# Turning a tile's normalised rows with transposing transfers in place of TensorE

## The reference

```python
def block(x, ...):                       # x: (2, 4096, 512) float32
    h = layernorm(x)                     # time mix
    k, r = h @ Wk.T, h @ Wr.T
    y = wkv_scan(-exp(time_decay), time_first, k, r)   # recurrence along the 4096 steps
    x = x + (sigmoid(r) * y) @ Wo.T
    z = layernorm(x)                     # attention and experts
    h = rmsnorm(z, gamma1)
    q = (h @ Wq + bq).reshape(b, t, 16, 32)
    kv = ((h @ Wdown + bdown) @ Wup + bup).reshape(b, t, 16, 64)
    att = softmax(q . k / sqrt(32))      # over the 16 heads of one token
    z = z + (att @ v) @ Wo2 + bo
    h2 = rmsnorm(z, gamma2)
    gate = softmax(h2 @ Wg + bg)         # 8 experts, all of them used
    return x + z + sum_e gate[e] * (h2 @ We[e])
```

## Time and profile before

| what | value |
|---|---|
| median of 3 runs | 2760.3 us (2759.11 to 2760.59) |
| the profiled execution's own time | 2758.6 us |
| its span, first to last instruction | 2756.5 us |
| TensorE busy | 2586.4 us (94%) |
| VectorE busy | 2133.6 us (77%) |
| ScalarE busy | 1531.3 us (56%) |
| GpSimd busy | 948.9 us (34%) |
| mean granted TensorE clock | 0.975 of full |
| queue of the transfers | 116.18 MB in 845,092 packets, 22.9% of the 16 engines' span |

### The profile page before, as it was taken

One profiled execution on the slowest core, in us unless ns is written; L12 is line 12 of the kernel. 1 busy time (PEld: TensorE's weight loads), 2 busy tenths in 40 slices (PEclk: granted clock), 3 DMA queues, 4 the chain that ended last, 5 costly groups with the idle time before them and its releaser, 6 DMA issues.

```text
span 2756.5 us, 48625 instructions
## 1 busy us (share of the span) xinstructions
PE 2586.4 (94%) x18896; PEld 1580.4 (57%) x18896; DVE 2133.6 (77%) x3647; ACT 1531.3 (56%) x2799; POOL 948.9 (34%) x970
## 2 busy tenths in 40 slices
PE   2458999999999999999999999999999999999999
PEld 2345566666556666655666665566666556655554
DVE  6677887788888778788877878887787888767743
ACT  5875555555555555555555555556555555654540
POOL 0453433333333333243333324333332433332420
PEclk7768999999999999999999999999999999999999
DMA  7202222211222221122222112222112222201220
GB/s 229 39 12 39 47 47 47 32 27 37 47 47 47 47 30 28 38 47 47 47 47 25 33 38 47 47 47 47 23 33 40 47 47 47 46 12 37 39 32 16
DMA packets 845322, 119.29 MB, mean 43 GB/s; under 512 B 813587, under 2 KB 813715, under 8 KB 845075
## 3 DMA queue, kind: packets, MB, share of 16 engines
q1 hardware_dynamic: 845092, 116.18, 22.9%
HBM read 48.49 MB, written 16.78 MB: 24 GB/s over the span
## 4 chain that ended last, share of the span: by engine, by line
PE 88%; DVE 4%; ACT 4%; POOL 2%; SPq 1%; issue 1%; DMA 0%; ACTq 0%; DVEq 0%; POOLq 0%
PE bank L1333 78%; PE bank L1355 3%; PE bank L1500 2%; PE bank L1471 2%; PE bank L1511 2%; DVE h2t L1104 1%; PE bank L1487 1%; POOL w_e L693 1%; ACT h2t L939 1%; PE bank L1512 1%; ACT ot L789 1%; DVE mcol L1234 0%; ACT t L888 0%; POOL pr L734 0%; DVE acc L1311 0%
## 5 line engine op out<-in xcount | busy, mean ns | idle before, releaser
L1333 PE MATMUL bank<-w_e,h2t 128*128 128x512 f16 x6144 | 1383.4, 380 | 2.8 <-DVE acc L1311 2.0
L1333 PEld LDWEIGHTS bank<-w_e,h2t 128*128 128x128 f16 x6144 | 592.1, 98 | 665.9 <-issue 4.4
L1311 DVE SCALAR_TENSOR_TENSOR acc<-bank,gates,acc 128x512 f32<-128x512 f32 x512 | 371.9, 736 | 120.4 <-PE bank L1333 117.4
L906 ACT ACTIVATE pr<-bank,plog,col 128x512 f32<-128x512 f32 x256 | 198.7, 776 | 407.9 <-PE bank L1500 405.5
L734 POOL TENSOR_TENSOR pr<-pr 128x512 f16<-128x512 f32 x256 | 295.7, 1160 | 182.3 <-ACT pr L908 180.9
L721 POOL TENSOR_TENSOR qo<-t,qo 128x256 f16<-128x256 f32 x128 | 106.5, 832 | 493.4 <-ACT qo L891 490.3
L1142 DVE TENSOR_TENSOR_SCAN wkv<-e,wkv 128x256 f32<-128x256 f32 x256 | 210.8, 864 | 74.6 <-ACT e L834 73.4
L1166 DVE RECIPROCAL zz<-zz 128x256 f32<-128x256 f32 x128 | 218.9, 1732 | 29.4 <-POOL zz L703 29.3
L1333 PE MATMUL bank<-w_o,xo 128*128 128x512 f16 x768 | 176.2, 387 | 46.9 <-DVE xo L1104 46.9
L908 ACT ACTIVATE pr<-bank,plog,col 128x512 f16<-128x512 f32 x256 | 197.8, 773 | 0.0
L1333 PE MATMUL bank<-xo,w_k 128*128 128x256 f16 x1536 | 172.9, 273 | 2.4 <-DVE xo L1104 2.4
(11 more groups left out here) (196 smaller groups left out, 3957.6 us busy)
## 6 DMA issues: line engine op xcount, KB each, us to landing
qs<-qo SPq DMA_DIRECT2D x384, 64.0 KB, 2.4
ks<-k SPq DMA_DIRECT2D x384, 64.0 KB, 2.4
xk<-in_attn_x SPq DMA_DIRECT2D x32, 512.0 KB, 4.0
x<-in_attn_x SPq DMA_DIRECT2D x32, 512.0 KB, 3.7
result<-acc SPq DMA_DIRECT2D x32, 512.0 KB, 2.8
w_e<-in_ffn_We SPq DMA_DIRECT2D x7, 1024.0 KB, 12.9
qs<-in_attn_Wk SPq DMA_DIRECT2D x1, 1024.0 KB, 7.9
ks<-in_attn_Wr SPq DMA_DIRECT2D x1, 1024.0 KB, 10.0
```

The costliest lines, as they stand in the source:

```text
L906: nc.scalar.activation(pr[:, k % 2, :], att_bank[ATT_BANK["S", k]][:, :], ACT.Exp, bias=plog[:, 0:1], scale=colof["soft"])\
L1311: V.scalar_tensor_tensor(out=acc[:, s, :], in0=moe_bank[u % 2][:, :], scalar=gates[:, s, e:e + 1], in1=acc[:, s, :], op0=ALU.mult, op1=ALU ...
L1333: ins = nc.tensor.matmul(dst, left(a), right(b), start=(n == 0), stop=(n == last))
```

## The change

For time mix and attention, TensorE's turn goes. The rows are split first, while tokens are on partitions: ScalarE writes the high half of each 128 rows and VectorE the low half, into `row16` (the storage of `v32`) and `hr16` (the storage of `k16`). SyncE then issues one transposing transfer for each half of each 128 rows, 4 for `mix_turn` and 4 for `att_turn`, 128x512 float16 (128 KB) each, from there to `xo16` and `ht16`. `mix_k` and `att_latent` on TensorE wait for the transfers (`turn_in`, `turn1_in`) and not for the low half. The turn of the second norm (`fin_turn2`) stays on TensorE. The bank ring of attention loses its two "T" uses. All order lists are new.

```diff
+            def mix_turn(t, _):                                    # SyncE
+                if t.back(1):
+                    sp.wait_ge(*mix_pe.done(t.back(1), "O"))
+                for s in range(SUB):
+                    for l, (steps, step) in enumerate(((mix_act, "x_hi"), (mix_dve, "x_lo"))):
+                        sp.wait_ge(*steps.done(t, step, s))
+                        sp.dma_start(xo16[:, l, :, s * P:(s + 1) * P], row16[:, l, s, :], transpose=True).then_inc(turn_in.sem, 16)
...
+            def att_turn(t, _):                                    # SyncE
+                if t.back(1):
+                    sp.wait_ge(*att_dve.done(t.back(1), "vt"))
+                for s in range(SUB):
+                    for l, (steps, step) in enumerate(((att_act, "h_hi"), (att_dve, "h_lo"))):
+                        sp.wait_ge(*steps.done(t, step, s))
+                        sp.dma_start(ht16[:, l, :, s * P:(s + 1) * P], hr16[:, l, s, :], transpose=True).then_inc(turn1_in.sem, 16)
...
             def mix_turn(t, _):                                    # ScalarE
-                for b in range(2):
-                    act.wait_ge(*mix_pe.done(t, "T", b))
-                    if b == 0 and t.back(1):
-                        act.wait_ge(*mix_pe.done(t.back(1), "O"))
-                    nc.scalar.activation(xo16[:, 0, 2 * b:2 * b + 2, :], mix_bank[b][:, :], ACT.Copy, scale=XS)\
-                        .then_inc(mix_act.sem, 1)
+                if t.back(1):
+                    act.wait_ge(*mix_dve.done(t.back(1), "e2v_1"))
+                for s in range(SUB):
+                    act.wait_ge(*pre_act.done(t, "norm", s))
+                    nc.scalar.activation(row16[:, 0, s, :], xk_rows[:, s, :], ACT.Copy, scale=XS).then_inc(mix_act.sem, 1)
...
             def mix_turn(t, _):                                    # VectorE
-                for b in range(2):
-                    dve.wait_ge(*mix_act.done(t, "x_hi", b))
-                    lo(xo16[:, 1, 2 * b:2 * b + 2, :], mix_bank[b][:, :], XS, xo16[:, 0, 2 * b:2 * b + 2, :]).then_inc(mix_dve.sem, 1)
+                for s in range(SUB):
+                    dve.wait_ge(*mix_act.done(t, "x_hi", s))
+                    lo(row16[:, 1, s, :], xk_rows[:, s, :], XS, row16[:, 0, s, :]).then_inc(mix_dve.sem, 1)
...
-            def mix_turn(t, _):                                    # TensorE
-                if not t.back(1):
-                    pe.wait_ge(ident_in, 16)
-                pe.wait_ge(*pre_act.done(t, "norm"))
-                turn(xk_rows, mix_bank, mix_pe, mix_pe.sem, lambda b: mix_free(t, "T", b))
...
             def mix_k(t, _):
-                pe.wait_ge(*mix_dve.done(t, "x_lo"))
+                pe.wait_ge(*turn_in.done(t, "x"))
```

More of the change, by code:

```diff
@@ L166 @@
+    ("att_probs", 1, 2), ("att_scores", 3, 2), ("moe", 6, 3), ("att_probs", 2, 2), ("att_scores", 4, 2),
+    ("att_probs", 3, 2),
 ]
 PE_TAIL = [
-    ("att_scores", 4, 4), ("moe", 7, 5), ("att_probs", 3, 4), ("att_scores", 5, 4), ("moe", 8, 5),
-    ("att_probs", 4, 4), ("att_scores", 6, 4), ("att_probs", 5, 4), ("att_scores", 7, 4), ("mix_project", 0, 3),
-    ("moe", 9, 5), ("mix_turn", 0, 2), ("att_probs", 6, 4), ("att_probs", 7, 4), ("moe", 10, 5), ("mix_k", 0, 2),
-    ("mix_v", 0, 2), ("att_turn", 0, 3), ("fin_project", 0, 4), ("att_latent", 0, 3), ("att_q", 0, 3),
@@ new lines @@
+    ("att_probs", 3, 3), ("att_scores", 5, 3), ("moe", 7, 4), ("att_probs", 4, 3), ("att_scores", 6, 3),
+    ("mix_project", 0, 2), ("att_probs", 5, 3), ("att_scores", 7, 3), ("moe", 8, 4), ("att_probs", 6, 3),
+    ("att_probs", 7, 3), ("moe", 9, 4), ("moe", 10, 4), ("mix_k", 0, 1), ("mix_v", 0, 1), ("att_latent", 0, 2),
+    ("att_q", 0, 2), ("fin_project", 0, 3), ("att_up", 0, 2), ("moe", 11, 4), ("moe", 12, 4), ("moe", 13, 4),
+    ("moe", 14, 4), ("moe", 15, 4), ("fin_turn2", 0, 3), ("att_max", 0, 2), ("att_max", 1, 2), ("fin_gate", 0, 3),
@@ new lines @@
+    ("mix_value", 1, 1), ("mix_scan", 1, 1), ("pre_stats", 0, 2), ("mix_rec", 2, 1), ("mix_rec", 3, 1),
+    ("mix_gate", 1, 1), ("att_probs", 1, 0), ("att_probs", 2, 0), ("att_probs", 3, 0), ("mix_split", 1, 1),
+    ("att_probs", 4, 0), ("pre_norm", 0, 2), ("mix_project", 0, 1), ("att_probs", 5, 0), ("att_probs", 6, 0),
+    ("mix_turn", 0, 2), ("att_probs", 7, 0), ("att_stats", 0, 1), ("att_norm", 0, 1), ("mix_decay", 0, 2),
+    ("att_turn", 0, 1), ("fin_back", 0, 0), ("mix_sum", 0, 2), ("att_latent", 0, 1), ("mix_value", 0, 2),
@@ new lines @@
+    ("mix_gate", 1, 2), ("att_probs", 2, 3), ("att_probs", 3, 3), ("mix_split", 1, 2), ("moe", 6, 4),
+    ("pre_norm", 0, 1), ("mix_project", 0, 2), ("mix_turn", 0, 1), ("att_probs", 4, 3), ("att_probs", 5, 3),
+    ("moe", 7, 4), ("moe", 8, 4), ("att_probs", 6, 3), ("att_probs", 7, 3), ("att_stats", 0, 2), ("att_norm", 0, 2),
+    ("att_turn", 0, 2), ("fin_back", 0, 3), ("mix_decay", 0, 1), ("moe", 9, 4), ("mix_sum", 0, 1),
+    ("att_latent", 0, 2), ("moe", 10, 4), ("mix_value", 0, 1), ("mix_scan", 0, 1), ("fin_project", 0, 3),
@@ L309 @@
+    ("att_scores", 7, 4), ("att_norm", 0, 3), ("att_turn", 0, 3), ("mix_k", 0, 2), ("fin_back", 0, 4),
+    ("mix_v", 0, 2), ("mix_exp", 0, 2), ("att_latent", 0, 3), ("att_q", 0, 3), ("mix_num", 0, 2), ("att_up", 0, 3),
+    ("mix_split", 0, 2), ("att_vt", 0, 3), ("fin_square", 0, 4), ("fin_norm2", 0, 4), ("fin_turn2", 0, 4),
+    ("moe_gate", 0, 4), ("att_rest", 0, 3), ("mix_exp", 1, 2), ("att_scores", 0, 3),
 ]
 ACT_TAIL = [
-    ("att_scores", 0, 5), ("mix_num", 1, 4), ("att_scores", 1, 5), ("att_scores", 2, 5), ("att_scores", 3, 5),
@@ new lines @@
+    ("att_scores", 7, 5), ("att_norm", 0, 4), ("att_turn", 0, 4), ("mix_k", 0, 3), ("fin_back", 0, 5),
+    ("mix_v", 0, 3), ("mix_exp", 0, 3), ("att_latent", 0, 4), ("att_q", 0, 4), ("mix_num", 0, 3), ("att_up", 0, 4),
+    ("mix_split", 0, 3), ("att_vt", 0, 4), ("fin_square", 0, 5), ("fin_norm2", 0, 5), ("fin_turn2", 0, 5),
+    ("moe_gate", 0, 5), ("att_rest", 0, 4), ("mix_exp", 1, 3), ("att_scores", 0, 4), ("att_scores", 1, 4),
+    ("att_scores", 2, 4), ("att_scores", 3, 4), ("mix_num", 1, 3), ("att_scores", 4, 4), ("mix_split", 1, 3),
@@ new lines @@
+    ("att_scores", 5, 4), ("pre_norm", 0, 2), ("att_scores", 6, 4), ("mix_turn", 0, 2), ("att_scores", 7, 4),
+    ("att_norm", 0, 3), ("att_turn", 0, 3), ("mix_k", 0, 2), ("fin_back", 0, 4), ("mix_v", 0, 2), ("mix_exp", 0, 2),
+    ("att_latent", 0, 3), ("att_q", 0, 3), ("mix_num", 0, 2), ("att_up", 0, 3), ("mix_split", 0, 2), ("att_vt", 0, 3),
+    ("fin_square", 0, 4), ("fin_norm2", 0, 4), ("fin_turn2", 0, 4), ("moe_gate", 0, 4), ("att_rest", 0, 3),
+    ("mix_exp", 1, 2), ("att_scores", 0, 3), ("att_scores", 1, 3), ("att_scores", 2, 3), ("att_scores", 3, 3),
@@ new lines @@
+    ("mix_num", 1, 2), ("att_scores", 4, 3), ("mix_split", 1, 2), ("att_scores", 5, 3), ("pre_norm", 0, 1),
+    ("att_scores", 6, 3), ("mix_turn", 0, 1), ("att_scores", 7, 3), ("att_norm", 0, 2), ("att_turn", 0, 2),
+    ("mix_k", 0, 1), ("fin_back", 0, 3), ("mix_v", 0, 1), ("mix_exp", 0, 1), ("att_latent", 0, 2), ("att_q", 0, 2),
+    ("mix_num", 0, 1), ("att_up", 0, 2), ("mix_split", 0, 1), ("att_vt", 0, 2), ("fin_square", 0, 3),
+    ("fin_norm2", 0, 3), ("fin_turn2", 0, 3), ("moe_gate", 0, 3), ("att_rest", 0, 2), ("mix_exp", 1, 1),
```

392 lines of the change are left out of this document (180 added, 212 removed), and 7 rows, old and new, of the table POOL_HEAD.

## The result

The changed kernel takes 2767.49 us (median of 9 runs, 2761.64 to 2776.26) against 2759.11 us (9 runs, 2757.44 to 2760.59) for the kernel before on the same chip: 1.0031 of its time, 95% interval 1.0020 to 1.0041. It is slower by 0.3%, a little over what a measurement can tell, where 2712 us and a gain were forecast. The profiled execution took 2768.87 us, its span is 2766.7.

What follows compares the result with a forecast made beforehand. TensorE, busy 2586 of 2756.5 us, was taken as the bound: 1.6 us gained a round over 30 tiles is 48, leaving 2708.5; 2.1 around the span and 1.7 to the median make 2712, range 2694 to 2850.

Steps and rivals of the forecast that it cites:

- the transfers: Loop, SyncE's queue: transposing transfers at 1.5 us each land 0.8 us before `mix_k` and 1.3 before `att_latent` are due.
- The bounds of 0.71 and 1.53 from the stacks' rows: One transposing transfer: at least 0.71 us, a 64 KB stack transfer's issue interval; 1.53 us in pieces of 64 bytes.
- The estimate of 3120 us: Late-transfer case: 1309 ns per block makes a transfer 5.2 us, the stall 14 us a tile; chance 1 in 20.
- Its walk: Loop, VectorE's new list walked with trace durations: split ends at 78.9 us, so a round of 79.0, gain 1.6 of 1.93.
- The rival in which it takes the place: Loop: VectorE's idle time doesn't shrink and it bounds the round; one more microsecond of waits gives 2751 us; chance 0.10.
- What is behind them on SyncE (the stacks, then the store, then loads) is due later: Loop, SyncE's queue behind the transposing transfers: nothing is late, as q is not there until after `att_q`; no cost priced.
- I take both at zero, with 8 us to either side: Head and tail: no net gain or loss from the change, with 8 us to either side.
- 2 to 4 us for each of four sets in a waiting chain: Head: what a transfer costs more than a turn where the chain waits; head and tail still taken at zero.
- The tail: End of the kernel: bound by TensorE like the loop; taken at zero together with the head.
- a forecast between 2697 and 2735 us: Whole kernel, likeliest case: rounds of 78.7 to 79.5 us; chance 0.58.
- The prediction's last line: Unpriced causes: a head over 8 us longer, or transposing transfers that slow the stacks.
- late transfers: Loop rival: TensorE waits for the transposing transfers, rounds of 83.0 us and 2832 us, or 84.1 and 2865; chance 0.32.

Runs made afterwards that it cites:

- e8_old_lists: The kernel before with both turns by transposing transfers, its own lists kept on TensorE, VectorE, ScalarE and GpSimd; 3114.9 us, 1.1286 of the kernel before.
- e1_stack20: The changed kernel without the last four of 24 stack transfers (k's low half) from tile 3 on, so less work; 2740.5 us, 0.9928 of the kernel before.
- e6_act_queue: The changed kernel with four of each tile's 24 stack transfers (q's high half) issued by ScalarE; 2748.7 us, 0.9962 of the kernel before.
- e10_act_turn: The changed kernel with four stack transfers a tile and the first tile's four transposing transfers on ScalarE's queue; 2738.2 us, 0.9922 of the kernel before.
- e5_k_first: The changed kernel with `mix_k` and `mix_v` ahead of expert 10 and `fin_project` behind `att_up`; 2759.8 us, 0.9999 of the kernel before.
- e4_head: The changed kernel with three moves in its head lists: first transposing transfers, experts' scales and six weight scalings sooner; 2770.6 us, 1.0038 of the kernel before.
- e9_late_experts: The changed kernel with four stack transfers on ScalarE, experts 4 to 7 prepared later, first turn sooner, tail `fin_project` sooner; 2749.4 us, 0.9964 of the kernel before.
- e3_att_only: The kernel before with only attention's turn by transfers, lists kept but for the moves needed; 2770.9 us, 1.0039 of the kernel before.

## Why the prediction was wrong

**Right: the transfers.** One takes 1.30 us of queue (1.5 was taken) and lands 2.5 us after its issue, and nothing of it shows in the loop: `mix_k` starts 14.06 us behind `mix_project` (13.8), `ht` is there for `att_latent` at 24.5 (24.3). The bounds of 0.71 and 1.53 from the stacks' rows held it. That 1.5 came so near is in part luck: 1.53 went by pieces of 64 bytes, but the transfers made 544 pieces each, which at the prediction's 11.95 ns would be 0.41 us. By the profile's page, 29.0% of 16 engines' span where 22.9% was, the 256 transfers held the engines for some 0.67 us each (an estimate from rounded shares), so for about half of the 1.30 us the engines are not what the queue waits for. The Trainium skill's rate in "DMA: Bandwidth & Descriptors" (latency and other measured facts), 261 GB/s, is not borne out: 128 KB every 1.30 us is 101 GB/s. Nor is the 1309 ns for one 128x128 block of "VectorE: DVE Perf Modes" (three transpose paths), if it is taken for each block of a queue of them: here 1.30 us is the issue of four blocks. The estimate of 3120 us that hung on it is near the 3114.9 us of e8_old_lists by luck, since the mechanism there is another: too early a due time, and the clock.

**Right: VectorE.** Its walk gave a round of 79.0 with `mix_decay` 0 at 21.7, 1 at 46.5 and the split at 78.9; the trace has 21.95, 46.7 and 79.19, and the good rounds take 79.24. The split ends 0.06 us before TensorE goes on to the next `mix_project`, so VectorE has nothing to spare, as foreseen, and costs at most the 0.24 us by which the good rounds miss 79.0. The rival in which it takes the place did not come.

**The step that failed.** "What is behind them on SyncE (the stacks, then the store, then loads) is due later: q is not there until after `att_q`". It looked at the stacks as something behind the transposing transfers and not at their own due time. The new list puts `mix_k` at 13.8, where it was 9.27 behind `mix_project` before (1072.99 - 1063.72), and all that follows moves with it: q comes at 33.5 instead of 29.7, and `att_max` does not move back as far: without a wait it starts at 51.84 (e1_stack20), 50.51 before. The kernel before had 0.7 to 2.0 us to spare there. Its SyncE queue and TensorE, end of the chain that the earlier trace rows begin:

```profile
1027.10 2.82 SPq L659 DMA_DIRECT2D ks<-k  x4
```

```profile
1033.65 1.06 PE L1487 MATMUL bank<-ks,qs 104*128 104x128 f16 x16
```

The last issue ends at 1029.92 and `att_max` starts at 1033.65 without a wait; in the changed kernel 1.75 us lie between the two (1138.69 to 1140.44), the time that the transfer takes to land. So the slack was 3.73 - 1.75 in this round, which is one of the best. In the next, one issue takes 1 us longer, and 2.71 - 1.75 = 0.96 us are left:

```profile
1093.41 6.69 SPq L655 DMA_DIRECT2D qs<-qo  x8
...
1108.72 2.81 SPq L659 DMA_DIRECT2D ks<-k  x4
```

```profile
1114.24 1.06 PE L1487 MATMUL bank<-ks,qs 104*128 104x128 f16 x16
```

The trace of before had the price too: 24 issues of 0.71 us and 2.4 us to landing, 33.5 + 17.1 + 1.7 = 52.3, with `att_max` due at 51.84. That is 0.5 us late with nothing going wrong. But 17.1 us is the shortest chain: in 15 of the 25 rounds, before and after alike, it takes 17.75 to 18.4, which by the same sum is 1.2 to 1.9 us late. It cost 1.01 us a round, 25 us in all, of which a part is the clock: e1_stack20 shows it by a shorter chain, e6_act_queue and e10_act_turn by a shorter chain with all the transfers, e5_k_first by an earlier q (the wait goes, and another comes). The transposing transfers did not slow the stacks: the chain takes 17.72 us in the mean, 17.75 before.

**Also failed: "I take both at zero, with 8 us to either side".** The head lost 25.1 us. The prediction's 2 to 4 us for each of four sets in a waiting chain would have made 8 to 16 of it. The runs show that the first transfers' place behind the loads costs some 3.5 us up to the first `mix_project` (87.1 in e4_head for 90.6, 86.0 in e10_act_turn for 89.4 in e6_act_queue), against a spread of 2.0; the rest of the wait in front of `mix_k` 0 only moved (TensorE waits 45.88 us for VectorE's `xo` in e4_head, 38.10 in the changed kernel); that the 26.85 us wait on ScalarE is its preparation of experts, which can be moved but not won (e9_late_experts); and that a turn by transfer costs some 8 us in the head even with the old order (e3_att_only, attention's alone). Up to the second `mix_project` most of the loss, 13.8 of 19.8 us, comes with the transfers even in the old lists (e8_old_lists). How the 5 us behind it are shared stays open, since that kernel's rounds bear waits of their own there.

**The tail** was taken to be like the loop, and from the 29th `mix_project` on the kernel gained 6.5 us: the last three rounds gained 14.5 (254.3 to 239.8), and the end behind the last `mix_project` lost 8.0 (149.1 to 157.1). The wait of 7.43 us for the last `ht` is in that end; two orders tried in its place lost 7.0 and 4.7 us to VectorE.

The sum: 48 us of gain forecast and 10.2 of loss measured, 58 apart. 25 of it is the head, 25 x (80.26 - 79.0) = 31.5 the rounds; of those 25 the stacks and 6 the 0.25 us by which even the best rounds miss 79.0. The rest, 2, is in the last rounds. The chance for a forecast between 2697 and 2735 us was too high because the stacks' due was not priced at all and the head's at nothing. (Its upper end is 2732 by its own terms: 2760.3 - 1.2 x 30 + 8.) The prediction's last line had named both as causes without a price, a head over 8 us longer and slower stacks; the first came as it says, the stacks came late without being slower. That 2767.5 us lies between 2694 and 2850 is luck, since that range was opened upward for late transfers, which did not come.
